# A Mamba mixer's silu visits on ScalarE: two decays and a conv tap of the next unit ahead of each, three decays behind it

## What is computed

```python
xz = x_in @ W_in                      # 512 -> 2 x 1024
x, z = jnp.split(xz, 2, axis=-1)
x = silu(conv4(x) + conv_b)           # depthwise, 4 taps
Bm, Cm = jnp.split(x @ W_x, 2, axis=-1)          # 16 states each
delta = jax.nn.softplus(x @ W_dt + b_dt)
# for each of 1024 channels d and 16 states s, along time:
#   h = exp(delta * A[d, s]) * h + delta * B[s] * x
#   y[d] = sum over s of h * C[s]
y = (y + x * D) * silu(z)
out = y @ W_out + residual
```

## Time and profile before

| | us |
|---|---|
| median of three runs (lowest to highest) | 5149.2 (5144.1 to 5151.3) |
| the profiled execution's own time | 5146.8 |
| its span on the core | 5144.9 |
| first scan to last scan of the mixer | 739.2 to 4521.5 |
| VectorE waits for a decay of ScalarE, whole run | 135.3 + 124.5 |

### The profile page before, as it was taken

The page is one execution under the profiler, slowest core; times in us unless marked ns, Lnnn a source line. Parts: engine busy times, 40 slices in busy tenths (PEclk is TensorE's granted clock), DMA queues, the critical chain, the costliest instruction groups (busy, mean ns, idle before and its releaser), DMA issues. The chain is left out here.

```text
span 5144.9 us, 68121 instructions
## 1 busy us (share of the span) xinstructions
PE 4680.2 (91%) x20608; PEld 3107.8 (60%) x20608; DVE 4427.8 (86%) x5590; ACT 3284.4 (64%) x6613; POOL 3723.6 (72%) x1269
## 2 busy tenths in 40 slices
PE   8999987989989998999989898989899988889999
PEld 6777755555555555555555555555555555468887
DVE  6777659999999999999999999999999998967775
ACT  4656536666767767766767666767767666644443
POOL 1111029999999999999999999999999999921110
PEclk9999999999999999999999999999999999989999
DMA  3222341433343442424343424334342434121111
GB/s 84 83 89 74 115 154 39 136 104 126 103 138 105 136 138 94 153 87 146 99 135 101 136 94 143 114 125 140 96 146 92 141 103 143 58 82 50 66 58 41
DMA packets 374241, 549.07 MB, mean 107 GB/s; under 512 B 37488, under 2 KB 176752, under 8 KB 373872
## 3 DMA queue, kind: packets, MB, share of 16 engines
q1 hardware_dynamic: 135920, 286.65, 16.5%
q10 hardware_dynamic: 237952, 258.00, 15.8%
HBM read 472.19 MB, written 72.38 MB: 106 GB/s over the span
## 5 line engine op out<-in xcount | busy, mean ns | idle before, releaser
L1024 POOL TENSOR_TENSOR mx_dbu<-mx_bs,mx_du 128x2048 f32<-128x2048 f32 (+1 forms) x513 | 2323.4, 4530 | 147.2 <-DVE mx_hp L1368 144.4
L1237 ACT ACTIVATE mx_ps_da<-mx_dl,mx_a 128x512 f32<-128x512 f32 x2048 | 1403.4, 685 | 89.4 <-issue 32.5
L1368 DVE TENSOR_TENSOR_SCAN mx_ps_da<-mx_ps_da,mx_hst,mx_dbu 128x512 f32<-128x512 f32 x936 | 1198.9, 1282 | 107.5 <-ACT mx_ps_da L1237 98.5
L1499 PE MATMUL mx_ps_m<-mx_u,mx_w_d 128*128 128x512 f32 x2048 | 1001.5, 624 | 95.9 <-ACT mx_gy L1142 92.7
L1041 POOL TENSOR_TENSOR mx_hp<-mx_hp,mx_w_in 128x1024 f32<-128x1024 f32 x400 | 942.7, 2357 | 54.6 <-ACT mx_hst L1200 54.6
L1368 DVE TENSOR_TENSOR_SCAN mx_hp<-mx_ps_da,mx_hst,mx_dbu 128x512 f32<-128x512 f32 x600 | 758.4, 1264 | 90.8 <-ACT mx_ps_da L1237 90.7
L1537 PEld LDWEIGHTS mx_ps_y<-mx_ident,mx_hp 128*128 128x128 f32 x3200 | 387.4, 142 | 504.5 <-POOL mx_hp L1041 299.1
L1380 DVE TENSOR_TENSOR mx_hc<-mx_ps_da,mx_w_in 128x512 f32<-128x512 f32 x1024 | 687.4, 671 | 3.6 <-DVE mx_hp L1368 0.7
L1220 ACT ACTIVATE mx_hst<-mx_ps_da 128x1 f32<-128x1 f32 x1023 | 173.3, 169 | 804.6 <-DVE mx_hc L1380 796.9
L1499 PEld LDWEIGHTS mx_ps_m<-mx_u,mx_w_d 128*128 128x128 f32 x2048 | 377.3, 199 | 455.4 <-issue 350.1
L1537 PE MATMUL mx_ps_y<-mx_ident,mx_hp 128*128 128x128 f32 x3200 | 499.2, 279 | 153.4 <-POOL mx_hp L1041 152.8
(11 more groups left out here) (134 smaller groups left out, 7423.8 us busy)
## 6 DMA issues: line engine op xcount, KB each, us to landing
mx_w_o<-in_L_attn_W_out ACTq DMA_DIRECT2D x480, 256.0 KB, 3.9
mx_w_d<-in_L_attn_W_dt ACTq DMA_DIRECT2D x128, 512.0 KB, 4.2
mx_bs<-bc_scratch SPq DMA_DIRECT2D x128, 512.0 KB, 4.8
mx_w_in<-bc_scratch SPq DMA_DIRECT2D x128, 512.0 KB, 6.4
mx_w_z<-w_in_scratch ACTq DMA_DIRECT2D x128, 256.0 KB, 2.6
mx_w_u<-w_in_scratch ACTq DMA_DIRECT2D x120, 256.0 KB, 2.7
mx_hT<-hT_scratch SPq DMA_DIRECT2D x16, 1030.0 KB, 5.9
hT_scratch<-f_h2T SPq DMA_DIRECT2D x16, 1024.0 KB, 8.7
```

Of the source, the lines that this page charges most:

```text
L1024: G.tensor_tensor(dbu[:, n % NM:n % NM + k].rearrange("p n s t -> p (n s) t"), bs[:, g:g + k].rearrange("p n s t -> p (n s) t"), bcast(du[ ...
L1237: ins = A.activation(ps_da[DA_BANK[p]][:, k, :], dl[:, b % NL, :], ACT.Exp, scale=a_sb[:, b, s:s + 1])
L1368: V.tensor_tensor_scan(da if in_psum(p) else hp[:, n % NH, 0, :], da, dbu[:, n % NM, s, :], 0.0 if first else hst[:, b, SG * g + s:SG * g ...
L1499: ins = M.matmul(ps_m[1][:, :], w_d[:, k, :], u[:, cp, k, :], start=(k == 0), stop=(k == ND - 1), skip_group_check=True)
```

## The change

Around the visit of unit n, ScalarE now makes both decays of unit n + 1 ahead of the visit (it made one), and the first conv tap of unit n + 1 as well. Behind the visit it makes three decays at once (both of unit n + 2 and half 0 of unit n + 3), with the copy `keep` of unit n between them. VectorE multiplies by C between its two scans in units n and n + 2 (it did so in n + 1), so that a PSUM buffer comes free in time. In the tables, the conv products move from units 3 and 7 of each eight to units 1 and 6 and TensorE makes them first in their unit; the gate projection moves from 4 to 5; the three parts of the delta projection from 6, 7, 0 (4, 1 and 3 blocks of weights) to 7, 0, 1 (4, 2 and 2); softplus from 2 and 3 to 3 and 4; GpSimd's two steps from 5 and 6 to 6 and 7; turning back and gating from 5 and 6 to 6 and 0; output products, weight loads and copies shift by a unit or so. No operation is added or removed.

```diff
-        IN_AT = [NG // 2 * q - NU - 13 for q in range(NI)]
-        GATE_AT = [NG * b - 12 for b in range(ND)]
-        DT_AT = [NG * b + d for b in range(ND) for d in (-10, -9, -8)]
+        IN_AT = [NG * b - NU + d for b in range(ND) for d in (-15, -10)]
+        GATE_AT = [NG * b - 11 for b in range(ND)]
+        DT_AT = [NG * b + d for b in range(ND) for d in (-9, -8, -7)]
...
-        RELU_AT = [NG * b - 6 for b in range(ND)]
+        RELU_AT = [NG * b - 5 for b in range(ND)]
...
+        def visit_in(n):
+
+            return n in Z_SILU_AT
+
+        def around_visit(p):
+
+            return any(2 * at + 2 <= p <= 2 * at + 6 for at in Z_SILU_AT)
+
+        def c_between(n):
+
+            return any(n in (at, at + 2) for at in Z_SILU_AT)
...
                     for half in range(2):
-                        if before_visit(n) and half == 0:
-                            continue
-                        decay(i, 2 * n + half)
+                        if not around_visit(2 * n + half):
+                            decay(i, 2 * n + half)
...
-                    if due(Z_SILU_AT, n, i):
+                    if visit_in(n):
+                        decay(i, 2 * n + 2)
+                        decay(i, 2 * n + 3)
+                        first_taps(i, par, n + 1)
                         A.preload_act_table_set("silu_and_others")
                         for k, s in due(Z_SILU_AT, n, i):
                             silu_z(i + s, (par + s) % 2, k)
                         for k, s in due(U_SILU_AT, n, i):
                             silu_u(i + s, (par + s) % 2, k)
                         A.preload_act_table_set("natural_log_exp_and_others")
+                        decay(i, 2 * n + 4)
+                        decay(i, 2 * n + 5)
+                        keep(i, n)
+                        decay(i, 2 * n + 6)
...
-                    if before_visit(n):
+                    if c_between(n):
                         times_c(i, n)
                     scan(i, n, 1, first)
```

More of the change, by code:

```diff
@@ L813, in mixer_phase @@
         YT_AT = [NG * b + NG + 5 for b in range(ND)]
-        BACK_AT = [NG * b + NG + 5 for b in range(ND)]
-        YG_AT = [NG * b + NG + 6 for b in range(ND)]
-        OUT_AT = [NU + n for n in (-6, -5, -3, -3, 1, 1, 2, 9,
[3 rows of a table removed]
+        BACK_AT = [NG * b + NG + 6 for b in range(ND)]
+        YG_AT = [NG * b + NG + 8 for b in range(ND)]
+        OUT_AT = [NU + n for n in (-6, -6, -5, -5, -4, -2, 2, 10,
[3 rows of a table added]
         RES_AT = [NU - 7] + [OUT_AT[ND * j - 1] + 2 for j in range(1, TJ)]
         EVAC_AT = [OUT_AT[ND * (j + 1) - 1] + 2 for j in range(TJ)]
-        WU_AT = [NG * b - 80 for b in range(ND)]
-        WZ_AT = [NG * b - 18 for b in range(ND)]
-        WD_AT = [NG * b - 14 for b in range(ND)]
+        WU_AT = [NG * b - 81 for b in range(ND)]
+        WZ_AT = [NG * b - 17 for b in range(ND)]
+        WD_AT = [NG * b - 13 for b in range(ND)]
         WO_AT = [n - NU + 1 for n in OUT_AT[-NW:]] + [n + 1 for n in OUT_AT[:-NW]]
@@ L837, in mixer_phase @@
         NE = len(ALL_IN_PSUM)
-        def before_visit(n):
-            return any(n % NU == (at + 1) % NU for at in Z_SILU_AT)
+        def visit_in(n):
[4 more added lines that the diff above has]
+            return any(n in (at, at + 2) for at in Z_SILU_AT)
         def in_psum(p):
@@ L1269, in prologue, with first_taps @@
                         silu_u(c, c, k)
+            def first_taps(i, par, n):
+                for q, s in due(IN_AT, n, i, TAPS):
+                    first_tap(i + s, (par + s) % 2, q)
             def body(i, par, first):
@@ L1276, in body @@
                     for half in range(2):
-                        if before_visit(n) and half == 0:
-                            continue
-                        decay(i, 2 * n + half)
-                        if half == 0 or before_visit(n):
+                        if not around_visit(2 * n + half):
+                            decay(i, 2 * n + half)
+                        if half == 0:
                             for bb, s in due(RELU_AT, n, i):
                                 relu(i + s, bb)
-                            for q, s in due(IN_AT, n, i, TAPS):
-                                first_tap(i + s, (par + s) % 2, q)
+                            if not visit_in(n - 1):
+                                first_taps(i, par, n)
                             for bb, s in due(YT_AT, n, i):
@@ L1287, in body @@
                                 skip(i + s, (par + s) % 2, bb)
-                    if n >= KEEP_LAG:
-                        keep(i, n - KEEP_LAG)
-                    elif not is0(i):
-                        keep(i - 1, NU + n - KEEP_LAG)
-                    if before_visit(n + 1):
-                        decay(i, 2 * n + 2)
+                    if n == 0 and not is0(i):
+                        keep(i - 1, NU - 1)
+                    elif n > 0 and not visit_in(n - 1):
+                        keep(i, n - 1)
                     for bb, s in due(GATE_AT, n, i, ZCOPY):
@@ L1429, in body @@
                     taps(i, par, n, 2)
-                    if not before_visit(n):
+                    if not c_between(n):
                         times_c(i, n)
@@ L1586, in body @@
                             last_out_product(j, b0, b1)
+                    for q, s in due(IN_AT, n, i):
+                        input_product(i + s, (par + s) % 2, q)
                     for m, s in due(OUT_AT, n, i):
@@ L1596, in body @@
                         gate_product(i + s, (par + s) % 2, b)
-                    for q, s in due(IN_AT, n, i):
-                        input_product(i + s, (par + s) % 2, q)
                     if n >= SUM_LAG:
```

20 lines of the change are left out of this document (10 added, 10 removed), and 6 rows, old and new, of the table OUT_AT.

## The result

| | before | after |
|---|---|---|
| median of four runs (lowest to highest), us | 5150.2 (5144.1 to 5152.4) | 5223.2 (5216.5 to 5232.5) |
| first scan to last scan of the mixer, us | 739.2 to 4521.5 | 740.9 to 4593.8 |

The changed kernel is slower: the ratio is 1.0145, with an interval of [1.0126, 1.0164]. I had forecast 5055. Of the 73 us, 71 lie in the mixer, which grew from 3782.3 to 3852.9.

A forecast was written before the change was run, and what follows sets the result against it. VectorE's own work, plus a piece of ScalarE's at each visit, was taken to set the mixer's pace. A gain of 1.43 us times 64 is 92, plus 6, less 4: 5149 - 94 = 5055 us, range 5015 to 5115.

The forecast's parts named there:

- (c): Softplus copy, gate product and taps elsewhere: cost nothing while ScalarE, busy for 41.38 of 59.63 us, has idle time.
- the sum: Gains and costs per visit net 1.43 us; times 64 is 92, plus 6 makes 98, less 4 for GpSimd.
- The first wait: VectorE's wait for a decay just behind the visit: 1.57 us against 1.93, a gain of 0.36 per visit.
- The second wait: VectorE's next decay wait behind a visit: 0.2 us on the mean against about 1.6, gain 1.4 per visit.
- (a): VectorE's multiply right behind its own scan costs 1.32 us instead of 1.19; one in the open, 0.13 per visit.
- (b): The output buffer's copies move from unit 35 to 36: about 0.9 us once in a chunk, 0.2 per visit.
- (d): At a chunk's end a tap fills some 0.4 of VectorE's 0.96 us wait: 6 us gained in all.
- taken at 4 us: GpSimd has little room, so 4 us were taken off the gain of 98.
- The tap ahead of the visit: Rival: this tap waits for TensorE's conv product beyond 2.1 us of slack; 5 us late gives 5240; chance 0.09.
- GpSimd did not take over: Rival: late `keep` delays GpSimd's dbu, VectorE waits about 0.7 us per stretch: 45 us, 5100; chance 0.15.
- nothing changes: Rival: waits return at units 20 and 21 as delayed softplus delays delta, taking all 1.4 us per visit; chance 0.06.
- The slower side: Slower than before: 0.09 for the tap waiting for TensorE and 0.01 for a worse return of waits, 0.10.

The follow-up runs named there:

- e15: The changed kernel with 25 output weight loads per chunk on SyncE's queue and product 4 at unit 62: 5073.5 us, ratio 0.9857 to before.
- e1: The changed kernel with the old table of output products, its loads and copies following from it: 5111.8 us, ratio 0.9931 to before.
- e3: The kernel before with the new order around the visit alone, all tables old: 5149.9 us, ratio 1.0001 to before.
- e7: e1 with the copy `keep` behind the first of the three decays after the visit: 5088.0 us, ratio 0.9883 to before.
- e8: e1 with TensorE's transposes of the SBUF states one unit later: 5076.4 us, ratio 0.9859 to before.
- e17: e15 with the copy `keep` behind the first decay after the visit: 5071.3 us, ratio 0.9852 to before.
- e18: e17 with TensorE's transposes one unit later: 5070.8 us, ratio 0.985 to before.

## Why the prediction was wrong

**The step that failed** is (c) under what the change adds: softplus, gate and taps elsewhere "cost nothing", because VectorE waits for none of them now. It lists the moved steps without the output products and their weight loads, which the section on the change had passed over as shifting "by a unit or so". No term of the sum held them, and no rival. The weight loads have two faults there. First, a product that moves a unit earlier while its buffer's last user moves a unit later loses two units: products 14, 20 and 30 had three units between load and use, and now have one; product 4 had six and has one. Second, the load of `w_d` moved into the units of just these loads: a load of the output's weights right behind it took 4.5 us to land (median of 99), a load with no other transfer beside it 2.6 (63). The three weight loads behind the visit were in my working, but only as 0.57 us of ScalarE's time. When they land, and who waits for that, was not asked. For the steps that (c) does list it held: in e15 VectorE waits 49.9 us for taps, 48.7 before. Taking the product table back gives 111 us (e1), and loads in time with product 4 two units later give 150 (e15).

**The first wait** was right: 1.57 forecast, 1.57 in the row at 1530.12, and 1.51, 1.60, 1.69 and 1.69 on the mean of twelve chunks at units 3, 19, 35 and 51. e15 has 1.35, 1.59, 1.55 and 1.74. The exact hit at unit 17 is in part luck: the other visits are up to 0.2 off.

**The second wait** was forecast as 0.2 on the mean; it is 0.28 at unit 20 and nothing at the three others, and nothing at all in e15.

**(a) The multiply behind its own scan** was sized too low. VectorE's time without waits was to grow by 0.5 us per chunk (0.13 times 4). By its timeline over twelve chunks it grows from 220.6 to 221.5 in e15, to 222.4 in e1 and to 222.8 in the changed kernel. In e15 the time from a scan's start to the multiply behind it is 1185 ns on the mean of the 62 in a chunk, instead of 1175, and from a tap to the scan behind it 408 instead of 385 on 32. Over all that is 15 us in e15, where 8 were in the sum.

**(b) The copies of unit 36** come with a wait of 0.75 us per chunk at unit 37. Before, there was one of 0.23 at unit 36, so they cost 0.5, against 0.9 forecast. The first tile's copies moved to unit 12 in the same way, which the sum left out: 0.71 at unit 13, against 0.49 at unit 12 before. Both together cost 0.7.

**(d) The tap at a chunk's end** did its part: VectorE's waits in unit 0 fall from 1.45 us to 0.82 in the changed kernel. In e15 they are 1.54. Of these only 0.66 are for a decay (1.18 before), but 0.73 are for `dbu`, so that GpSimd takes back what the tap gives.

**GpSimd** was taken at 4 us. In e15 VectorE waits 27.8 us for `dbu`, before 3.7. Not all of these 24 us are a loss, since some stand where a decay was waited for before, but this rival was nearer than the sum had it.

**The sum without the failed step.** In e15 VectorE's waits per chunk fall from 16.7 to 11.1, 90 us over 16 chunks, its own work grows by 15, and 75 us remain: less than the forecast's 94, inside its range and by its mechanism. The misses cancel in part, which is luck: the waits at the four visits fall by 8.0 us per chunk where 7.0 were forecast, and the terms above take more than they were given. The stretch of the visit of unit 17 takes 57.73 us, where 58.1 was forecast.

**The rivals.** The tap ahead of the visit did not wait for TensorE: the row at 1524.12 starts right behind its decay, and of 60 such taps 58 wait 0.14 us or less (the two others, 7.6 and 1.1 us, stand at the mixer's start). GpSimd did not take over, and "nothing changes" was true only of e3, where the waits came back at the taps. The slower side had a chance of 0.10, all on mechanisms that did not occur.

**The Trainium skill** gives on "ScalarE: Activation LUTs", section "What ACT_TABLE_LOAD costs", a drain of about 1380 ns for a switch. The rows after disagree with it as those before did: the decay behind the second load starts 1.30 us after the load does (1528.00 and 1529.30).

What stays open is what does away with the price of TensorE's wait for GpSimd in e15. That it is gone is shown by e7 and e8 (24 and 35 us) against e17 and e18 (3 us). Whether the order of the products or SyncE's queue does it is not told apart. For the order speaks that VectorE's waits for TensorE in e1 stand at units 14, 18, 26, 42 and 62, each right behind a pair of products (units 13, 17, 25, 41 and 61; behind the six other pairs there is none over 0.15 us per chunk), and that TensorE's wait for GpSimd is as long in e15 as in e1. But the new table has pairs as well, at other units, and why these do no harm is open.
